# Attention over 32 batches: PV in two blocks of two units, a third probability buffer, the second transposition of the maxima one head later

## What is computed

```python
# layer 0 (low-rank terms folded into q and v), no mask
attn = softmax(q @ k.T * ATTN_SCALE, axis=-1)
out = (attn @ v) @ w_proj + b_proj
# layer 2: q and k rotated (RoPE), causal mask
att = where(causal, (q @ k.T) * scale, min); att = softmax(att, axis=-1)
y = (att @ v) @ w_proj
```

## Time and profile before

| | |
|---|---|
| median of three executions | 1470.41 us (1470.06 to 1474.22) |
| the profiled execution | 1472.95 us, its span 1471.2 us |
| PE busy | 1124.8 us, 76% |
| DVE busy | 1085.5 us, 74% |
| ACT busy | 843.2 us, 57% |
| POOL busy | 553.4 us, 38% |

### The profile page before, as it was taken

How to read it: one execution, slowest core, us unless ns; L and a number is a source line. 1 busy time by engine, 2 the same in 40 slices (tenths; PEclk the granted TensorE clock), 3 DMA queues, 4 the chain that set the end, 5 groups by cost and what they waited for, 6 DMA issues and landing times. The chain is left out here.

```text
span 1471.2 us, 36081 instructions
## 1 busy us (share of the span) xinstructions
PE 1124.8 (76%) x11411; PEld 782.7 (53%) x11411; DVE 1085.5 (74%) x2949; ACT 843.2 (57%) x1844; POOL 553.4 (38%) x572
## 2 busy tenths in 40 slices
PE   2599999999999996128999999999999957203220
PEld 1366666666666653016777777777777734102120
DVE  1479999999999976515676777767777756898996
ACT  1267777777777663615666666666666635203554
POOL 5323323333233303364444554445544232002555
PEclk9899999999999998558999999999999988655555
DMA  5545554545545413044444544444444302000111
GB/s 144 140 115 119 119 132 111 131 111 127 125 115 133 100 34 118 14 100 102 109 114 109 116 110 112 108 113 115 107 116 101 81 16 93 7 0 1 30 36 50
DMA packets 115921, 137.26 MB, mean 93 GB/s; under 512 B 12112, under 2 KB 101520, under 8 KB 106640
## 3 DMA queue, kind: packets, MB, share of 16 engines
q1 hardware_dynamic: 112704, 132.25, 37.1%
q10 hardware_dynamic: 3152, 4.20, 1.1%
HBM read 85.03 MB, written 37.75 MB: 83 GB/s over the span
## 5 line engine op out<-in xcount | busy, mean ns | idle before, releaser
L353 DVE TENSOR_REDUCE attn_negmax<-attn_row_ps 128x2 f32<-128x512 f32 (+1 forms) x1024 | 607.0, 618 | 238.7 <-PE attn_row_ps L535 226.3
L297 ACT ACTIVATE attn_probs<-attn_col_ps 128x512 f32<-128x512 f32 (+1 forms) x1024 | 540.3, 547 | 243.3 <-PE attn_col_ps L557 226.7
L535 PE MATMUL attn_row_ps<-attn_k_st,attn_q_st 72*128 72x256 bf16 (+1 forms) x2048 | 369.9, 262 | 16.9 <-DMA attn_k_st<-attn_scratch 15.2
L557 PE MATMUL attn_col_ps<-attn_q_st,attn_k_st 74*128 74x256 bf16 (+1 forms) x2048 | 370.6, 262 | 2.4 <-ACT attn_probs L297 1.0
L574 PE MATMUL attn_out_ps<-attn_probs,attn_v_sb 128*32 128x256 f32 (+1 forms) x4096 | 250.0, 362 | 1.3 <-ACT attn_probs L297 1.3
L557 PEld LDWEIGHTS attn_col_ps<-attn_q_st,attn_k_st 74*128 74x128 bf16 x2048 | 180.2, 99 | 92.6 <-ACT attn_probs L297 31.6
L535 PEld LDWEIGHTS attn_row_ps<-attn_k_st,attn_q_st 72*128 72x128 bf16 x2048 | 202.0, 99 | 42.8 <-issue 16.6
L282 POOL TENSOR_TENSOR attn_rstd<-attn_var,minus_half 128x2 f32<-128x2 f32 x64 | 45.5, 711 | 386.4 <-DVE attn_var L418 386.4
L531 PE MATMUL attn_row_ps<-mask_qk,ident_h 128*128 128x256 bf16 x512 | 141.0, 276 | 24.4 <-DMA attn_k_st<-attn_scratch 23.9
L574 PEld LDWEIGHTS attn_out_ps<-attn_probs,attn_v_sb 128*32 128x32 f32 x4096 | 107.4, 109 | 87.4 <-issue 22.5
L553 PE MATMUL attn_col_ps<-mask_kq,ident_h 128*128 128x256 bf16 x512 | 141.8, 277 | 14.6 <-DMA attn_q_st<-attn_mT_sb 11.9
(11 more groups left out here) (229 smaller groups left out, 1682.1 us busy)
## 6 DMA issues: line engine op xcount, KB each, us to landing
attn_q_st<-attn_scratch SPq DMA_DIRECT2D x192, 192.0 KB
attn_k_st<-attn_scratch SPq DMA_DIRECT2D x192, 192.0 KB
attn_scratch<-attn_parts SPq DMA_DIRECT2D x64, 384.0 KB, 3.0
attn_scratch<-attn_parts SPq DMA_DIRECT2D x64, 128.0 KB, 3.1
attn_x_in<-in_L_attn_x_dram SPq DMA_DIRECT2D x32, 128.0 KB, 2.2
moe_xs<-x_all SPq DMA_DIRECT2D x8, 512.0 KB, 3.1
attn_x_in<-x_mid SPq DMA_DIRECT2D x32, 128.0 KB, 2.1
ffn_xs<-x_mid SPq DMA_DIRECT2D x16, 256.0 KB, 2.3
```

The lines of the kernel that those rows point to most:

```text
L297: nc.scalar.activation(probs[:, u % 2, j, 0:W], col_ps[:, n % 2, 0:W], ACT.Exp, scale=scale).then_inc(probs_kept, 1)
L353: nc.vector.tensor_reduce(negmax[:, t, 2 * p:2 * p + 2], row_ps[:, row_bank(st, u), 0:2 * keys].rearrange("p (a k) -> p a k", a=2), AX_X, ...
L535: last = nc.tensor.matmul(bank[:, a * keys:(a + 1) * keys], q_st[0:KROWS, sl, h, t * P:(t + 1) * P], k_st[0:KROWS, sl, h, 0:keys], start=n ...
L557: last = nc.tensor.matmul(bank[:, t * N:(t + 1) * N - first], k_st[0:rows, sl, h, t * P:(t + 1) * P], q_st[0:rows, sl, h, first:N], start= ...
```

## The change

The table `AT` gets new positions, PV is given as a table of blocks (head: lag and units) and the probabilities get three buffers.

- PV: units 0 and 1 of lag 3 behind head 9, units 2 and 3 of lag 4 behind head 1, in both attentions. Before: units 0, 1, 2 of lag 3 behind heads 6, 10, 14, and unit 3 of lag 4 behind head 3 (attn0) or 2 (attn1).
- attn0: the second transposition of the maxima and the q/k projection go from PE's head 2 to 3, the v projection from 4 to 5; ACT's copy of these maxima goes from head 1 to 2, that of q and k from 2 to 3, that of the PV sums from 3 to 2. In attn1 these stay where they were.
- The probabilities are `probs[:, (4 * batch + u) % 3]`; a unit's first exponential waits for unit u-3.

```diff
-AT = {"attn0": dict(act_xT=0, act_mT1=1, act_qk=2, act_oT=3, act_onT=8, act_mT0=11,
+AT = {"attn0": dict(act_xT=0, act_mT1=2, act_qk=3, act_oT=2, act_onT=8, act_mT0=11,
                     dve_o=6, dve_split0=8, dve_v=7, dve_y=13, dve_var=14, dve_ln=15,
-                    pe_xT=0, pe_mT1=2, pe_pv3=3, pe_qk=2, pe_oT=5, pe_pv=6, pe_v=4, pe_onT=8, pe_mT0=10, pe_y=13),
+                    pe_xT=0, pe_mT1=3, pe_qk=3, pe_oT=5, pe_v=5, pe_onT=8, pe_mT0=10, pe_y=13,
+                    pe_pv={1: (4, (2, 3)), 9: (3, (0, 1))}),
       "attn1": dict(act_xT=0, act_mT1=0, act_qk=1, act_oT=2, act_onT=10, act_mT0=11,
                     dve_o=3, dve_split0=9, dve_v=5, dve_y=12, dve_var=14, dve_ln=15,
-                    pe_xT=0, pe_mT1=1, pe_pv3=2, pe_qk=1, pe_oT=4, pe_pv=6, pe_v=3, pe_onT=10, pe_mT0=11, pe_y=12)}
+                    pe_xT=0, pe_mT1=1, pe_qk=1, pe_oT=4, pe_v=3, pe_onT=10, pe_mT0=11, pe_y=12,
+                    pe_pv={1: (4, (2, 3)), 9: (3, (0, 1))})}
+PROBS = 3
...
-        probs = sb("probs", [P, 2, 4, 2 * N])
+        probs = sb("probs", [P, PROBS, 4, 2 * N])
...
+        def probs_of(st, lag, u):
+            return probs[:, (4 * (st.off - lag) + u) % PROBS, :, :]
...
-                            wait(act, pv_ready, st.seq(3, 4, u - 1))
-                        nc.scalar.activation(probs[:, u % 2, j, 0:W], col_ps[:, n % 2, 0:W], ACT.Exp,
+                            wait(act, pv_ready, st.seq(3, 4, u + 1 - PROBS))
+                        nc.scalar.activation(probs_of(st, 3, u)[:, j, 0:W], col_ps[:, n % 2, 0:W], ACT.Exp,
...
-                                                probs[:, u % 2, j, t * N:(t + 1) * N - first],
+                                                probs_of(st, lag, u)[:, j, t * N:(t + 1) * N - first],
...
                     if n == at["pe_mT1"] and st.has(3):
                         transpose_max(st, 3, 1)
-                    if n == at["pe_pv3"] and st.has(4):
-                        sum_values(st, 4, 3)
+                    if n in at["pe_pv"] and at["pe_pv"][n][0] == 4 and st.has(4):
+                        for u in at["pe_pv"][n][1]:
+                            sum_values(st, 4, u)
                     if n == at["pe_qk"] and st.has(0):
                         project_qk(st)
                     if n == at["pe_oT"] and st.has(4):
                         transpose_o(st)
-                    if n in (at["pe_pv"], at["pe_pv"] + 4, at["pe_pv"] + 8) and st.has(3):
-                        sum_values(st, 3, (n - at["pe_pv"]) // 4)
+                    if n in at["pe_pv"] and at["pe_pv"][n][0] == 3 and st.has(3):
+                        for u in at["pe_pv"][n][1]:
+                            sum_values(st, 3, u)
```

## The result

The changed kernel takes **1541.72 us** (median, 1538.41 to 1542.95) beside 1470.24 for the kernel before: 1.048 times as long, 95% interval 1.046 to 1.050. The profiled execution took 1542.66 us, span 1540.9; that of before 1472.95, span 1471.2. The span grew by 69.7 us; forecast were 65.

What follows compares the result with a forecast made beforehand. The prediction took attn1 to be bound by one chain through five engines, attn0 by PE and DVE sharing the step. Profiled 1472.95 us + 44 + 21 gave 1538, or 1535 us as a median 2.5 lower; range 1503 to 1551.

Steps and rivals of the forecast that it cites:

- 16.65 + 1.57: attn1: old step plus the full time of a two-unit PV block, 18.2 us a step, +44 us in all.
- The cycle: attn1: chain from head 0 through PE, ACT, POOL, SP and maxima DMA to next head 0, 16.82 us.
- the block: attn1: two PV units between head 0 and the projection, priced at 1.57 us, bounds 1.45 to 1.78.
- the walk: attn0: one step followed from PE's head 3, giving 16.0 us instead of 15.26, +21 us in all.
- The wait for DVE's output: attn0: PE waits 0.7 us at head 8 before transposing the normalised output.
- the wait for DVE's split: attn0: PE's 0.44 us wait before the second transposition of the maxima goes away.
- the third: attn0: maxima DMA lands 2.15 us after issue (1.7 to 2.34), putting head 0 at 12.5 us.
- Third buffer: Third probability buffer: costs nothing in time.
- (a): attn1 as forecast, but attn0 gains, its step 14.9 us: 1504 us in all; chance 0.14.
- (b): PE work decides in both attentions because attn1's chain is not closed: 24 us less, 1447 us; chance 0.05.
- (c): attn1's PE waits lose the clock, some 6 us a step at half rate, 3 us lost: 1619 us; chance 0.04.
- (d): No effect, PE's gain and the chain's loss cancel across the attentions: 1470 us; chance 0.03.

Runs made afterwards that it cites:

- e3: Changed kernel with attn1's block of units 2 and 3 behind head 2, after the q/k projection, instead of head 1: 1502.77 us, ratio 1.024.
- e5: Changed kernel with attn0's transposition of the normalised output and ACT's copy of it at head 9 instead of 8: 1551.17 us, ratio 1.054.
- e6: Changed kernel with attn0's first maxima transposition at head 9 instead of 10, ACT's copy at 9 instead of 11: 1545.67 us, ratio 1.053.
- e7: Changed kernel with the edits of e3, e5 and e6, and attn1's first-maxima DMA issued ahead of the two stores: 1497.84 us, ratio 1.018.
- e1: Changed kernel with attn0 at its old positions, attn1 as changed, three probability buffers kept: 1512.10 us, ratio 1.030.
- e2: Changed kernel with attn1's old PV blocks, attn0 as changed, three probability buffers kept: 1504.26 us, ratio 1.025.
- e10: e7 with the first-maxima DMA issued ahead of the stores in attn0 too: 1464.15 us, ratio 0.997.
- e12: e1 with attn1's maxima DMA before stores, second maxima transposition and q/k and v projections one head later, PV-sum copy one head earlier: 1454.19 us, ratio 0.990.
- e9: Changed kernel with the first-maxima DMA issued ahead of the two stores in both attentions: 1508.45 us, ratio 1.027.

## Why the prediction was right, and where it was off

**attn1, mechanism right, price off by a sixth.** Forecast 16.65 + 1.57, measured 18.03. The cycle, the part of it that stays (15.1) and the wait in its place (about 1.3, measured 1.18 at 917.91; over all steps 32.3 us in 26) are confirmed by the trace, and e3 confirms that the place of the block does it. The mis-sized term is the block: between head 0 and the projection it costs 1.31. I had added 0.10 for entering it and 0.12 for leaving it. But here it follows the 16-column transposition of the maxima (901.28), the first PV record stands at 901.29, and no gap is seen; the entry was in the step before the change already. The transposition begins 0.31 after the last score rows (900.97, 901.28), in before too, just as a PV block elsewhere in attn1 does (910.43, 910.74), where a plain next head follows after 0.22 (909.11, 909.33). That block takes 910.74 to 912.18, 1.44, and 0.10 to enter, near the 1.57 of the forecast. By steady steps that is 28 x 1.31 = 37; the measured +38.4 has the uneven early steps in it.

**attn0, the walk right in a quiet step, the mean not.** Counted from head 3 at 299.78, with the forecast in brackets: head 6 at 3.64 (3.5), transposition of the output 5.82 (5.7), head 10 at 8.49 (8.4), head 0 at 12.54 (12.5). Block of two: 308.27 - 306.41 = 1.86, with 0.09 to enter 1.95 (1.98). The wait for DVE's output is 0.49 (0.7). (The forecast calls the wait for DVE's split, which goes, 0.44, where its row shows 0.28; no term of the walk hangs on it.) The shortest steps take 15.99 to 16.00, exactly the forecast; the mean is 16.26, at the upper bound given. The step of the argument that failed is the third: "in attn1 the same issue takes 2.34 until PE starts ... here it may be 1.7 to 2.34". The landing was taken as a fixed time from the issue. It is the end of a second path (projection, ACT, POOL, stores, landing), in which the stores ahead count: in after, head 0 starts 2.0 to 2.7 us after the issue and the wait is anything up to 1.0. Nor are there fewer stores in front of it than in attn1: both attentions issue the same two. A step of 16.00 is one in which this path is just in time. The same mistake made the expectations of e5, e6 and e7 wrong by 20 to 56 us.

**The total** came out 6.7 us above 1535 and inside the range. Between the profiled executions it is 4.7: attn0 8.5 more, attn1 5.6 less, and 1.8 outside the counted steps. The rest is that the median of after lies 0.9 below its profiled execution and not 2.5, and rounding. That the total is so near is in part luck: the errors of the two attentions have opposite signs.

**Third buffer:** costs nothing in the steps, as said (15.19 and 16.65 with it, 15.21 and 16.66 without). The medians of e1 and e2 leave open a cost somewhere else.

**Rivals.** (a), attn0 takes the gain: no, 16.26 and not 14.9; even with both waits closed e10 stands at 15.57, with PE in part kept waiting by a DVE that its own block had starved. (b), PE work decides in attn1: no, by e3. The forecast's price for a pair was right, but the sparing bought nothing in any of the kernels run, on the cycle or off it (e12). (c), the clock: it came about in single steps. The trace of after early in attn1, PE by time and two stretches:

```profile
790.40 0.28 PE L559 MATMUL attn_col_ps<-mask_kq,ident_h 128*128 128x256 bf16 x1 [1.82 <-DMA attn_q_st<-attn_mT_sb]
```

```profile
788.00:790.00 2.00, 0.58 (x6) 0.27 (x4) 1.93 (x7) 0.77 (x2) 0.69 (x1) 1.00 0.55 154
...
792.00:794.00 2.00, 2.00 (x25) 1.41 (x27) 0.69 (x1) 0.74 (x2) 0.00 (x0) 0.50 0.00 0
```

The wait of 1.82 us is followed by a granted clock of 0.50, in a step of 19.51 us. It is the only full step of attn1 in after that lost the clock; the early ones of 19.17 and 18.82 were long at a clock of 1.00. Behind the regular waits of 1.14 and 1.18 the steps are 17.8 to 18.2 and the clock isn't lost. The length of the wait alone doesn't decide. Waits of 2.41 (until 717.48) and 1.77 us (until 754.01) in after and of 1.64 (until 387.57) in e5 were followed by no drop, and in e6 one of 1.18 was, PE by time and the stretch behind it:

```profile
343.75 0.39 PE L563 MATMUL attn_col_ps<-attn_q_st,attn_k_st 74*128 74x256 bf16 x2 [1.18 <-DMA attn_q_st<-attn_mT_sb]
```

```profile
344.00:346.00 2.00, 2.00 (x14) 1.18 (x16) 1.93 (x7) 1.55 (x3) 1.41 (x2) 0.58 0.00 0
```

So the forecast was right for the steady step of attn1, and thinner than it looked. The 4% given to this rival rested on one short wait that kept the clock, and a wait as long as the regular ones of attn1 lost it once. The Trainium skill, TensorE: Matmul & The Clock Gate, in its section on HAM oscillation, describes a wait in each turn that throttles each turn; in attn1 of after the waits are in each turn and the throttling is not. (d), the two cancel: no, both lost.

## What to carry to other kernels

Look for the cycle before you count an engine's work: follow one step from an instruction round through all engines to the same instruction of the next step, and price a moved piece by whether it stands inside. A small transfer that somebody waits for belongs ahead of the big stores of its queue: behind them it is issued only when they can be, and it lands about when they do. One such swap gave 1.2% where re-pairing PE's work gave nothing. Work that is spared on the busiest engine is only worth what its neighbours can use; a longer unbroken block on one engine is also a longer pause for those that it feeds.

## What the runs showed of the hardware

- The same maxima DMA was usable 2.0 us after its issue in front of the stores (e9), 2.9 to 4.9 when issued 1.1 to 1.8 behind the first of them (e6, e7).
- A drop of the granted clock to 0.50 followed waits of PE of 1.50 (e5) and 1.82 us (after) and lasted about 3 us. It followed one of 1.18 in e6, but none of the waits of 1.01 to 1.21 that after has in its later steps of attn1, nor its waits of 1.77 and 2.41. The rows of before had shown it only beside stretches of 2 us with PE busy for 0.24.
- Between a transposition with 16 output columns and the PV block with 32 (901.28 and 901.29) no seam shows; between the scores with 128 and either of them it is near 0.10.
